# A fused recurrence and linear-attention layer: rotated q and k turned by VectorE in 32x32 blocks, all scores in one bank

## The reference

```python
x = x + tanh(g_xattn[0]) * wkv(time_decay, time_first, layernorm(x), ctx_2048)
x = x + tanh(g_ffn[0]) * ffn(layernorm(x), conv_w, Wq, Wk, Wv, Wg, router_w, Wout)

# ffn, with H = 16 heads, q and k of 32 dims a head, v of 64
x = silu(x_prev * conv_w[:, 0] + x * conv_w[:, 1])
q = silu(x @ Wq); k = x @ Wk; v = x @ Wv; g = x @ Wg
q = apply_rotary(q, cos, sin); k = apply_rotary(k, cos, sin)
scores = softmax(einsum('bhld,hdr->bhlr', v, router_w)); onehot = one_hot(argmax(scores), 2)
norm = 1.0 / cumsum(onehot)                      # 0 where the sum is 0
q_exp = q * scores * onehot * norm; k_exp = k * onehot
qk = einsum('bhld,bhmd->bhlm', q_exp, k_exp) * 32 ** -0.5 * tril
o = einsum('bhlm,bhmd->bhld', qk, v)
o = (o - mean(o)) / sqrt(var(o) + 1e-5)          # per head
out = (silu(g) * o) @ Wout
```

## Time and profile before

| | |
|---|---|
| median of 3 runs (lowest, highest) | 1722.92 us (1722.74, 1723.07) |
| the profiled execution: time, span | 1723.12 us, 1721.3 us |
| mean granted TensorE clock | 0.975 |
| busy: PE, DVE, ACT, POOL | 92%, 85%, 44%, 38% of the span |
| chain that ended last | PE 87%, DVE 8% |

### The profile page before, as it was taken

How to read it: one execution, slowest core, us unless ns; L and a number is a source line. 1 busy time by engine, 2 the same in 40 slices (tenths; PEclk the granted TensorE clock), 3 DMA queues, 4 the chain that set the end, 5 groups by cost and what they waited for, 6 DMA issues and landing times.

```text
span 1721.3 us, 37826 instructions
## 1 busy us (share of the span) xinstructions
PE 1584.1 (92%) x15863; PEld 824.3 (48%) x15863; DVE 1457.5 (85%) x2014; ACT 754.0 (44%) x965; POOL 661.9 (38%) x716
## 2 busy tenths in 40 slices
PE   0425999999999999999999999999999999999996
PEld 0112455555555555555555555555555555555552
DVE  7889888888898888888998888888988888889832
ACT  4825444444434444444444444444344444444420
POOL 1421344433344444333344444333444443333421
PEclk9957999999999999999999999999999999999998
DMA  9500011110010111111101111100101111101000
GB/s 270 198 13 1 26 38 38 38 38 26 26 36 28 37 38 38 38 30 29 32 27 37 38 38 38 38 26 26 37 26 38 38 38 38 35 26 30 14 14 25
DMA packets 23417, 70.78 MB, mean 41 GB/s; under 512 B 2256, under 2 KB 2512, under 8 KB 23248
## 3 DMA queue, kind: packets, MB, share of 16 engines
q1 hardware_dynamic: 23248, 68.37, 13.7%
HBM read 51.59 MB, written 16.78 MB: 40 GB/s over the span
## 4 chain that ended last, share of the span: by engine, by line
PE 87%; DVE 8%; issue 2%; ACT 1%; POOL 1%; DMA 0%; SPq 0%; POOLq 0%; DVEq 0%; ACTq 0%
PE ps_g L388 25%; PE ps_g L389 25%; PE ps_g L392 25%; PE ps_o L549 4%; PE ps_t L380 3%; PE ps_o L380 2%; DVE big L795 2%; PE ps_t L534 1%; DVE seg L867 1%; PE ps_s L534 1%; PE ps_t L486 1%; DVE big L836 1%; PE ps_s L511 0%; DVE seg L858 0%; ACT big L612 0%
## 5 line engine op out<-in xcount | busy, mean ns | idle before, releaser
L388 PE MATMUL ps_g<-big,h_hi 128*128 128x512 f16 x1536 | 586.1, 382 | 6.2 <-DVE h_lo L1037 5.9
L389 PE MATMUL ps_g<-big,h_hi 128*128 128x512 f16 x1536 | 585.4, 381 | 0.0
L392 PE MATMUL ps_g<-big,h_lo 128*128 128x512 f16 x1536 | 585.1, 381 | 0.0
L392 PEld LDWEIGHTS ps_g<-big,h_lo 128*128 128x128 f16 x1536 | 150.9, 98 | 183.5 <-issue 3.9
L388 PEld LDWEIGHTS ps_g<-big,h_hi 128*128 128x128 f16 x1536 | 153.6, 100 | 174.4 <-issue 10.8
L389 PEld LDWEIGHTS ps_g<-big,h_hi 128*128 128x128 f16 x1536 | 150.9, 98 | 165.2 <-issue 3.5
L1193 POOL TENSOR_TENSOR small<-small 128x1 f32<-128x1 f32 x64 | 14.3, 223 | 560.9 <-DVE small L852 560.8
L388 PE MATMUL ps_g<-big 128*128 128x512 f16 x512 | 195.1, 381 | 0.7 <-DVE big L926 0.7
L389 PE MATMUL ps_g<-big 128*128 128x512 f16 x512 | 194.5, 380 | 0.0
L392 PE MATMUL ps_g<-big 128*128 128x512 f16 x512 | 194.4, 380 | 0.0
L1212 POOL TENSOR_TENSOR vx<-vx,ek 128x1024 f32<-128x1024 f32 x32 | 75.4, 2355 | 288.2 <-ACT ek L621 278.3
(11 more groups left out here) (173 smaller groups left out, 2853.9 us busy)
## 6 DMA issues: line engine op xcount, KB each, us to landing
x_ring<-in_x SPq DMA_DIRECT2D x32, 512.0 KB
vx<-in_ctx SPq DMA_DIRECT2D x32, 512.0 KB
out<-x_ring SPq DMA_DIRECT2D x32, 512.0 KB
big<-in_wv SPq DMA_DIRECT2D x2, 2048.0 KB, 21.2
big<-in_wg SPq DMA_DIRECT2D x2, 2048.0 KB, 20.8
big<-in_wout SPq DMA_DIRECT2D x2, 2048.0 KB, 20.1
big<-in_wq SPq DMA_DIRECT2D x1, 2048.0 KB, 14.4
big<-in_wk SPq DMA_DIRECT2D x1, 2048.0 KB, 19.7
```

What stands on the lines that cost most here:

```text
L388: nc.tensor.matmul(dst[:, :], hi, hi_of(u)[:, kc * HALF:(kc + 1) * HALF], start=(kc == 0), stop=False)
L389: nc.tensor.matmul(dst[:, :], hi, lo_of(u)[:, kc * HALF:(kc + 1) * HALF], start=False, stop=False)
L392: last = nc.tensor.matmul(dst[:, :], lo, hi_of(u)[:, kc * HALF:(kc + 1) * HALF], start=False, stop=(kc == KC - 1))
```

## The change

Rotated q and k are no longer turned by TensorE (8 transposes of 128x128 a block) and copied out of `ps_t` by ScalarE. VectorE turns each of them by one block transpose of 128x512 in SBUF, `rot_q` to `q_sb` and `rot_k` to `k_sb`: every 32x32 block is turned in its place. So the dims of a head stand on the partitions of its own 32 tokens: token group n uses row tile n and column tile n for every head. All 64 scores go to one bank, `ps_s[0]`, in the order of `same_m` and `probs`, and one VectorE instruction masks all 512 columns. The semaphores `s_qtp` and `s_ktp` go; `s_qt` and `s_kt` are now VectorE's; `s_p` counts once a block instead of four times. TensorE's writes into `ps_t` and `ps_s[1]` are guarded by the readers that are left (`s_same`, `s_sgp`, `s_th`).

```diff
-        ps_sc = ps_t + ps_s
...
                     sign_sums(i)
-                    after(pe, s_rq, i + 1)
-                    transposes(ps_t[0], rot_q, s_qtp, as_is)
                     unit_ready(i, UV + 1)
...
                     after(pe, s_th, 2 * i + 1)
-                    after(pe, s_rk, i + 1)
-                    transposes(ps_t[1], rot_k, s_ktp, as_is)
                     same_route(i)
...
                 after(pe, s_gm2, p + 1)
-                after(pe, s_p, 4 * (p + 1))
+                after(pe, s_same, p + 1)
...
                 after(pe, s_us, i)
-                after(pe, s_p, 4 * i)
+                after(pe, s_same, i)
...
                     if main:
-                        after(pe, s_p, 4 * (n - 1) + g + 1)
+
+                        after(pe, s_sgp, n)
+                        after(pe, s_th, 2 * n - 1)
...
                 after(pe, s_kt, i + 1)
-                after(pe, s_p, 4 * i)
-                after(pe, s_same, i + 1)
+                after(pe, s_p, i)
...
             def scores(i):
 
-                for g in range(NG):
+                for h in range(H):
+                    tokens = slice(h * BLK, (h + 1) * BLK)
                     for n in range(NBLK):
-                        for h in range(HG):
-                            dims = slice(h * DK, (h + 1) * DK)
-                            tokens = slice(g * P + n * BLK, g * P + (n + 1) * BLK)
-                            last = nc.tensor.matmul(ps_sc[h][n * BLK:(n + 1) * BLK, g * BLK:(g + 1) * BLK],
-                                                    k_sb[dims, tokens], q_sb[dims, tokens], start=True, stop=True)
+                        dims = slice(n * BLK, (n + 1) * BLK)
+                        last = nc.tensor.matmul(ps_s[0][dims, tokens], k_sb[dims, tokens], q_sb[dims, tokens],
+                                                start=True, stop=True)
                 last.then_inc(s_sp, 1)
...
                     copy_v(i, 0)
                     if opening(i):
                         split_unit(5)
-                    act.wait_ge(s_qtp, i + 1)
-                    A(q_sb, ps_t[0][:, :], ACT.Copy).then_inc(s_qt, 1)
                     copy_v(i, 1)
                     if opening(i):
                         split_unit(6)
-                    act.wait_ge(s_ktp, i + 1)
-                    A(k_sb, ps_t[1][:, :], ACT.Copy).then_inc(s_kt, 1)
...
                     signs(i)
+                    turn_heads(s_rq, i, rot_q, q_sb, s_qt)
                     if opening(i):
                         lo_unit(4)
...
                     if opening(i):
                         lo_unit(6)
+                    turn_heads(s_rk, i, rot_k, k_sb, s_kt)
                     same(i)
...
                 if main:
-                    for h in range(HG):
-                        mask(i, h)
+                    mask(i)
...
                 dve.wait_ge(s_rt, i + 1)
-                dve.wait_ge(s_ktp, i + 1)
+                dve.wait_ge(s_kt, i + 1)
...
-            def mask(i, h):
-
+            def turn_heads(s_in, i, src, dst, s_out):
+
+                dve.wait_ge(s_in, i + 1)
+                V.transpose(dst, src).then_inc(s_out, 1)
+
+            def mask(i):
                 dve.wait_ge(s_sp, i + 1)
                 dve.wait_ge(s_same, i + 1)
-                if h == 0:
-                    after(dve, s_op, 2 * i)
-                of_tile = lambda m: m.rearrange("p (g h l) -> p g h l", h=HG, l=BLK)[:, :, h, :]
-                V.tensor_tensor(of_tile(probs), by_head(ps_sc[h][:, 0:P], BLK), of_tile(same_m), ALU.mult).then_inc(s_p, 1)
+                after(dve, s_op, 2 * i)
+                V.tensor_tensor(probs, ps_s[0][:, :], same_m, ALU.mult).then_inc(s_p, 1)
```

More of the change, by code:

```diff
@@ L210, in flamingo_layer @@
         s_qp, s_kp, s_vp, s_gp, s_up = sem("q_proj"), sem("k_proj"), sem("v_proj"), sem("g_proj"), sem("out_proj")
-        s_qtp, s_ktp, s_gtp = sem("q_transposed"), sem("k_transposed"), sem("gated_transposed")
+        s_gtp = sem("gated_transposed")
         s_cump, s_sp, s_op = sem("cum_matmul"), sem("scores_matmul"), sem("o_matmul")
@@ L226, in flamingo_layer @@
         s_r1q, s_r1k, s_rq, s_rk = sem("rot_q_part"), sem("rot_k_part"), sem("rot_q"), sem("rot_k")
-        s_qt, s_kt = sem("qt_copied"), sem("kt_copied")
+        s_qt, s_kt = sem("q_transposed"), sem("k_transposed")
         s_dlp, s_dlc, s_dl = sem("logits_matmul"), sem("logits_copied"), sem("route_logits")
@@ L523, in scores_ready @@
                 after(pe, s_kt, i + 1)
-                after(pe, s_p, 4 * i)
-                after(pe, s_same, i + 1)
+                after(pe, s_p, i)
             def scores(i):
-                for g in range(NG):
+                for h in range(H):
+                    tokens = slice(h * BLK, (h + 1) * BLK)
                     for n in range(NBLK):
-                        for h in range(HG):
-                            dims = slice(h * DK, (h + 1) * DK)
-                            tokens = slice(g * P + n * BLK, g * P + (n + 1) * BLK)
-                            last = nc.tensor.matmul(ps_sc[h][n * BLK:(n + 1) * BLK, g * BLK:(g + 1) * BLK],
-                                                    k_sb[dims, tokens], q_sb[dims, tokens], start=True, stop=True)
+                        dims = slice(n * BLK, (n + 1) * BLK)
+                        last = nc.tensor.matmul(ps_s[0][dims, tokens], k_sb[dims, tokens], q_sb[dims, tokens],
+                                                start=True, stop=True)
                 last.then_inc(s_sp, 1)
             def values_ready(i, g):
-                after(pe, s_p, 4 * (i + 1))
+                after(pe, s_p, i + 1)
                 after(pe, s_vc, 2 * i + g + 1)
```

## The result

The changed kernel takes 1711.95 us (median of 4 runs, 1711.15 to 1713.17) against 1722.99 us of the kernel before (4 runs). The ratio is 0.9935, 95% interval 0.9923 to 0.9947: faster by 0.65%. The profiled execution took 1711.15 us at a span of 1709.4 us.

What follows compares the result with a forecast made beforehand. A VectorE and ScalarE ring, hardly under TensorE's 48.73 us, was to bind: 48.73 - 0.86 + 0.45 + 0.05 = 48.37 us a period. With 29 periods, opening and end: 1712 us, range 1702 to 1723.

Steps and rivals of the forecast that it cites:

- The ring of VectorE and ScalarE: Middle blocks: closed cycle of waits through sum of squares, ratio, mask, convolution and silu; 48.11 us before, 48.37 after.
- The mask: Behind the gated values' split: one 128x512 mask and no wait for scores, 1.46 to 0.60 us, gain 0.86.
- The turn of q: VectorE's 128x512 transpose behind the route signs, ahead of carry copy and numerator: adds 0.45 us (bounds 0.30 to 0.80).
- the working: Numerator: L860 shifts 0.6 us, L322 runs alone, L1258 precedes the scan, L869 no longer waits, ends 0.45 us later.
- The list of signs: Middle: period 48.4 us, TensorE idle 0.5, mask and ratio without waits, scan near 2.4, L869 0.2, scores near 1.26.
- The turn of k: VectorE's transpose before L1055: 0.65 us with completion wait, covered by 0.60 us idle for ScalarE's polynomial; costs 0.05 us.
- need of 47.80 us: TensorE's chain per middle block: 48.73 us less 0.93 for eight dropped turns, scores unchanged.
- Where TensorE waits: Middle blocks: TensorE idle about 0.5 us each, before the output projection, released by VectorE's L926.
- Rival 1: TensorE's whole 0.93 us saving arrives in 31 blocks, the turns costing nothing; about 1694 us, chance 0.08.
- Rivals 2 and 5: 2: one-bank scores at 32 ns, about 1719 us, chance 0.10; 5: row tiles sharing a bank serialise, about 1960, 0.02.
- rival 3: No change: the ring's gain and cost cancel, for instance if the turn of q costs 0.8 us; 1720 to 1726, chance 0.12.
- Rival 4: Stretch L950 to L877: VectorE and POOL block each other once more, ring 49.2 us, run about 1737 us, chance 0.13.

## Why the prediction was right

**The bound.** The ring of VectorE and ScalarE was said to close at 48.11 us before and 48.37 after; the period is 48.29 to 48.34. The runs without turns and with TensorE's turn put back show that the ring sets the period after the change, and the run with the turns added to the kernel before shows its slack there. The part of the ring from the statistics of block i + 2 to the sum of squares, which the sum left as it was, got 0.04 to 0.08 us shorter; that was not foreseen. No run puts ScalarE's two copies back alone. That they were off the ring is read from before: behind the copy of q ScalarE is idle for 4.58 us until TensorE's projection is done, and behind the copy of k for 2.26 us until VectorE's L1002.

**The mask.** Said: 1.46 us to 0.60, a gain of 0.86. From the statistics (L843, L852 before) to the instruction behind the mask it was 801.43 - 798.64 = 2.79 us and is 798.24 - 796.36 = 1.88: 0.91. The 0.05 us more are in the split in front of the mask: its two halves take 1.15 us (796.49 to 797.64), where the prediction counted 1.20.

**The turn of q.** Said: 0.45 us, less than its own 0.6, since the order of POOL and VectorE tips. From the sum of squares to the end of the carry's copy it was 785.39 - 766.05 = 19.34 us and is 782.98 - 763.21 = 19.77: 0.43. The order of the waits is the one in the working: L321 is through in 1.27 us, L851 waits for it (1.89 us), L1252 gets in before the scan, the scan waits (3.15 us), the copy doesn't (0.22 us). The list of signs in the prediction contradicted that working at one point: it asked for "the scan near 2.4 us", though by the working the scan waits there for L1258's own time. It was the list that was wrong.

**The turn of k.** Said: 0.05 us, covered by the wait for the polynomial. Measured 0.13: from the carry's copy's end to the statistics the time grew from 13.25 to 13.38 us. The step that was mis-sized is the completion wait: `same` starts 0.81 us after the turn's start (789.71, 790.52), not 0.65. The cover was mis-sized too, by less: `same` and the idle time behind it took 1.28 us before (792.12 to 793.40), `same` alone takes 0.60 now (790.52 to 791.12), so the cover was 0.68 us and not 0.60. 0.81 - 0.68 is the 0.13.

**TensorE.** Its need of 47.80 us was right (47.81 busy), and so was that the scores keep their time. In the chain of waits they took 1.22 us before (799.37 to 800.59, where the next projection starts; the 1.26 us of the prediction end with the masks' release), and in one bank they take the same.

```profile
799.37 0.15 PE ps_t L534 x2
...
800.59 0.32 PE ps_g L388
```

```profile
1617.36 1.22 PE ps_s L529 x82
...
1618.68 0.38 PE ps_g L387
```

(The first two rows are of before. After, the next projection starts 0.10 us behind the scores' end, which is idle time of TensorE.)

That is where the trace and the Trainium skill (TensorEngine Tiling (Array Packing), "Gotcha 1: PSUM Pressure") differ: the page has it that different row tiles cannot access one bank at the same time; here four row tiles write one bank, each its own 32 partitions, and the 64 matmuls take no longer than into four banks. That they do overlap is shown by the run tile by tile, where each takes 60 ns in place of 19 at the same clock. The measurement decides, for this arrangement.

**Where TensorE waits** was wrong. Said: 0.5 us before the output projection, for the low part of the gated values. Of the 0.49 us, 0.10 stand there, behind the scores. The waits over 1100 us of the middle (us in total, times, longest) say that the rest is at the same-route matmul, 22 times, for VectorE's L952 (route coefficients, which free the bank and stand behind the whole numerator), and that a marked wait for L919 comes only 3 times:

```profile
PE ps_g L387 <- DVE small L952: 8.4, 22, 0.4
...
PE ps_g L387 <- DVE big L919: 1.1, 3, 0.5
```

(L387 is the projection behind the same-route matmul, whose own record is not in the trace.) Before, the turn of k, from 787.48 to 787.92, stood ahead of that matmul, later than the same instruction of VectorE. The time is not affected: L1047, which reads what the same-route matmul writes, has no idle mark, so this wait is off the ring.

**The ends.** The second block's statistics were said to be done at 216.0 us, 1.0 us later than before, and are done at 216.17. The last turns of x were said for 1622.0 and come at 1621.4, since the period is 0.03 us shorter than said.

```profile
215.96 0.21 DVE L843 BATCH_NORM_AGGREGATE small<-small 128x2 f32<-128x12 f32 x1
...
1621.43 0.87 PE ps_t L379 x8
...
1679.25 0.60 ACT big L639
```

The squares that open the tail start at 1679.25 against 1690.52, 11.3 us earlier, where 10.7 were said. The span is 11.9 us shorter: 0.6 us more came in the tail, which was said to be untouched. There TensorE begins the last projection, after the waits of the tail, at the lower clock, and in this execution it left it after three matmuls instead of six (mean granted clock of that projection 0.96, before 0.90). For the profiled execution the sum gives 1712.4 us, and 1711.15 were measured. That the median of 1711.95 is hit within 0.1 us is luck: in the ring small errors cancel (the turn of k cost 0.08 us more than said, the mask gained 0.05 more), and the profiled execution is the fastest of the four, 0.8 us under the median, where the prediction put it 0.2 us above.

**The rivals.** Rival 1 (TensorE's whole gain arrives) named 1694 us as its price; it is about what happens once the ring is relieved (1696.6 and 1696.85). Most of the difference is the opening: the rival counted TensorE's gain in the first two blocks too, 1.9 us, and without turns the first turns of x come only 0.3 us earlier (218.10, not 218.44). Rivals 2 and 5 fall with the scores' 1.22 us, rival 3 with the 0.43 us of the turn of q. Rival 4 (POOL and VectorE block each other once more) did not come, but the two moved transposes show that the place was the right one to fear: 11.7 us hang on one position there.

## What to carry to other kernels

Before work is taken off the busiest engine, close the next cycle of waits from the trace, engine by engine: mark each wait with whether the busiest engine ended it, and take out only those. Here that ring lay 0.6 us under TensorE's 48.7 us and gave 0.65% where TensorE's own work fell by 1.9%. And where two engines block each other, look for a tiny instruction that takes much longer than its own shortest time (here 1.04 us against 0.17): the difference is waiting, and an operation that takes no part in the blocking can be moved into it. Here that was worth as much again as the change (11.7 us and 11.0).

## What the runs showed of the hardware

- A VectorE block transpose from SBUF to SBUF was not slowed by POOL in the two places where other VectorE instructions had waited for it: 128x512 took 0.71 us while POOL's L313 ran, where a 16-column instruction had waited 0.9 us, and 128x1024 took 1.25 us (1.23 elsewhere) while POOL's product of gate and factor ran, where one with two inputs had waited 1.6 us.
- 64 fp32 matmuls of 32x32 into one bank take 1.22 us when neighbours stand on different diagonal tiles, and 3.86 us tile after tile at the same granted clock of 1.00 (up to 4.58 us where the clock falls within them).
- TensorE's granted clock fell to 1.2 GHz within such one-tile matmuls, though the engine is listed as busy without a gap. In the period with the scores from 788.35 to 792.93 it was 1.00 until 790, 0.76 from 790 to 792 and 0.50 from 792, and it was back at 1.00 from 798; the full-size matmuls in between started 0.43 us apart.
